# Edge counts of a four-layer graph network: windows of 64 destinations with source one-hots of 640 columns, interleaved with the first convolution's dense products

## The reference

```
h = max(layernorm(x), 0);  x = x + L0(h)     # one convolution: agg @ W_l.T + b_l + h @ W_r.T, relu
h = max(layernorm(x), 0);  x = x + L1(h)     # two convolutions of the same kind (mean over in-edges)
h = max(layernorm(x), 0);  x = x + L2(h)     # mean over out-edges, own layernorm inside
h = max(layernorm(x), 0);  x = x + L3(h)     # two GCN convolutions, self loops, 1/sqrt(degree)

agg = segment_sum(h[src], dst) / max(segment_sum(1, dst), 1)
```

## Time and profile before

| | |
|---|---|
| median of three executions | 733.56 us |
| span of the profiled execution | 731.7 us |
| TensorE busy | 706.2 us (97%) |
| VectorE busy | 433.6 us (59%) |
| ScalarE busy | 303.6 us (41%) |
| GpSimd busy | 31.0 us (4%) |
| counting and turning the counts | 13.9 to about 142 us |
| dense products of L0 | about 142 to 201 us |

### The profile page before, as it was taken

One profiled execution on the slowest core, in us unless ns is written; L12 is line 12 of the kernel. 1 busy time (PEld: TensorE's weight loads), 2 busy tenths in 40 slices (PEclk: granted clock), 3 DMA queues, 4 the chain that ended last, 5 costly groups with the idle time before them and its releaser, 6 DMA issues.

```text
span 731.7 us, 11918 instructions
## 1 busy us (share of the span) xinstructions
PE 706.2 (97%) x3435; PEld 551.0 (75%) x3436; DVE 433.6 (59%) x853; ACT 303.6 (41%) x613; POOL 31.0 (4%) x34
## 2 busy tenths in 40 slices
PE   3989999999999999999999999999999899999997
PEld 1545666688788888888888888888887678887786
DVE  5998999865456744422333466655699962247333
ACT  3887988522334222365311343222544352223321
POOL 1010111100000000000000000000222000000000
PEclk9999999999999999999999999999999999999999
DMA  7000000100012000011000201000200000000011
GB/s 245 5 1 15 20 24 30 57 0 0 2 59 73 0 0 1 6 69 58 0 0 1 74 4 54 1 0 0 74 0 0 2 2 0 1 0 0 32 57 54
DMA packets 12851, 18.68 MB, mean 26 GB/s; under 512 B 652, under 2 KB 5060, under 8 KB 12808
## 3 DMA queue, kind: packets, MB, share of 16 engines
q1 hardware_dynamic: 10472, 15.04, 6.3%
q10 hardware_dynamic: 2336, 3.08, 1.2%
HBM read 15.57 MB, written 2.56 MB: 25 GB/s over the span
## 4 chain that ended last, share of the span: by engine, by line
PE 78%; DVE 3%; issue 2%; ACT 1%; DVEq 0%; ACTq 0%
PE ps L1119 36%; PE ps L1161 36%; PE ps L1107 3%; PE ps L1063 2%; ACT cstage L485 1%; PE ps L1038 1%; PE ps L1022 0%; DVE own L890 0%; DVE countT L692 0%; DVE own L862 0%; DVE stats L658 0%; DVE own L795 0%; ACT apart L417 0%; DVE hT_lo L735 0%; DVE z L722 0%
## 5 line engine op out<-in xcount | busy, mean ns | idle before, releaser
L1161 PE MATMUL ps<-p_hi,cstage 128*128 128x512 f32 x600 | 234.5, 391 | 3.7 <-ACT cstage L485 2.0
L1161 PE MATMUL ps<-p_lo,cstage 128*128 128x512 f32 x600 | 233.6, 389 | 0.0
L1119 PE MATMUL ps<-w_hi,hT_hi 128*128 128x512 f32 x400 | 161.3, 403 | 2.1 <-DVE hT_lo L735 1.9
L1119 PE MATMUL ps<-w_hi,hT_lo 128*128 128x512 f32 x400 | 156.5, 391 | 0.0
L1119 PE MATMUL ps<-w_lo,hT_hi 128*128 128x512 f32 x400 | 156.0, 390 | 0.0
L1161 PEld LDWEIGHTS ps<-p_hi,cstage 128*128 128x128 f32 x600 | 112.6, 188 | 28.5 <-issue 5.3
L1161 PEld LDWEIGHTS ps<-p_lo,cstage 128*128 128x128 f32 x600 | 112.7, 188 | 23.1
L862 DVE SCALAR_TENSOR_TENSOR own<-ps,nodal,own 128x512 f32 (+1 forms) x60 | 44.9, 749 | 120.2 <-PE ps L1161 119.9
L1063 PE MATMUL ps<-src_hot,dst_hot 128*128 128x512 bf16 (+1 forms) x576 | 107.2, 345 | 6.3 <-DVE src_hot L675 5.4
L675 DVE TENSOR_SCALAR src_hot<-iota,nodeT 128x1250 bf16<-128x1250 f16 x192 | 94.2, 552 | 11.5 <-PE ps L1063 8.2
L485 ACT CAST cstage<-countT 128x1280 fp32r (+1 forms) x50 | 62.6, 1263 | 85.5 <-PE ps L1161 85.4
(11 more groups left out here) (124 smaller groups left out, 507.1 us busy)
## 6 DMA issues: line engine op xcount, KB each, us to landing
x<-in_x ACTq DMA_DIRECT2D x1, 2304.0 KB
out_x<-x SPq DMA_DIRECT2D x9, 256.0 KB
wstage<-in_L_gnn_W SPq DMA_DIRECT2D x2, 1024.0 KB, 5.2
vec<-in_L_gnn_b SPq DMA_DIRECT2D x4, 256.0 KB, 5.3
wstage<-in_L_gnn_W_r SPq DMA_DIRECT2D x4, 256.0 KB, 2.8
wstage<-in_L_gnn_W1l SPq DMA_DIRECT2D x1, 1024.0 KB, 5.1
wstage<-in_L_gnn_W1r SPq DMA_DIRECT2D x1, 1024.0 KB, 5.4
wstage<-in_L_gnn_W2l SPq DMA_DIRECT2D x1, 1024.0 KB, 5.3
```

Of the source, the lines that this page charges most:

```text
L1119: last = nc.tensor.matmul(ps[:, bank + r, :], a[:, r, k, :], w[:, slot, k, :], start=n == 0, stop=n == len(pairs) - 1)
L1161: last = nc.tensor.matmul(ps[:, AGG + r, :], cstage[:, part, k, :], p_[:, k, :], start=n == 1, stop=n == 2 * len(parts) * NT)
```

## The change

Six things change, all in the part up to the first aggregation.

1. Windows. Counting goes by 20 windows of 64 destinations (`WIN`, `NW`) instead of 10 blocks of 128. The sources are folded in two halves of 640: `src_hot` has 640 columns, and which half an edge belongs to goes into the sign of its destination, `(dst + 1) * (1 or -1)`. The 128 columns of `dst_hot` are then 64 destinations with the lower half of the sources and the same 64 with the upper half. TensorE multiplies two pieces of 320 columns. The minimum of two rounds to a block goes away; each window has at least one.
2. Who makes `dst_hot`. ScalarE makes the first three of a round (three `Abs`, one `Relu` over all three), GpSimd the last three with `is_equal` (`last_of_ring`).
3. Counts leave PSUM in four ScalarE activations of 64x640 to a block, straight into `count16`.
4. `countT16` is made by DMA: ten `dma_start_transpose` of 128x1280 on SyncE's queue, one when a block is complete. TensorE's and VectorE's share of the turning goes away. ScalarE and GpSimd wait for all ten before the first staging of an aggregation.
5. The two weights of L0 are loaded whole and transposed in two pieces of 16, before window 0 and between windows 0 and 1.
6. The products of L0 are interleaved: with block `b`, TensorE counts window 0, does the first product of tile `b-1`, counts window 1, transposes the features of tile `b` and does the second product of tile `b-1`.

```diff
-            def count(b, par, turned=None):
-                pe.wait_ge(counts_out, b + 1)
...
-                visits(n0, par)
-                if turned is not None:
-                    turn_counts(turned, par, GROUPS[2:])
-                    turn_first(turned, par)
...
+            def count(b, h, n1):
+
+                pe.wait_ge(counts_out, 2 * (2 * b + h) + 2)
...
+                with pe.Fori(n0, n1, RING) as n:
+                    for e in range(RING):
+                        if e == 0:
+                            pe.wait_ge(first_rows, n + 2 * RING)
+                        if e == HALF:
+                            pe.wait_ge(last_rows, n + 2 * RING)
+                        pe.wait_ge(givers_ready, n + e + 1)
+                        for k in range(2):
+                            last = nc.tensor.matmul(ps[:, COUNT + 2 * h + k, 0:NS // 2], dst_hot[:, e, :],
+                                                    src_hot[:, e, k * (NS // 2):(k + 1) * (NS // 2)], start=False,
+                                                    stop=False, skip_group_check=True)
+                        last.then_inc(hot_used, 1)
...
+            def merged(b, r):
+
+                n1 = visits_end(b)
+                count(b, 0, n1[0])
+                first_p(b - 1, 1 - r)
+                count(b, 1, n1[1])
+                turn(L0, b, r)
+                first_q(b - 1, 1 - r)
```

GpSimd's part, ScalarE's part and SyncE's transposes:

```diff
+            def last_of_ring(b, h, t0, t1, shift):
...
+                with pool.Fori(t0, t1, RING) as t:
+                    pool.wait_ge(last_rows, t + shift + RING)
...
+                    nc.gpsimd.tensor_copy(key_now[:, :], nodeT[:, 0, bass.ds(t + HALF, HALF)]).then_inc(key_set, RING)
+                    pool.wait_ge(key_set, t + shift + RING)
+                    pool.wait_ge(hot_used, t + shift + RING)
...
+                    for e in range(HALF):
+                        nc.gpsimd.tensor_scalar(dst_hot[:, HALF + e, :], tab_now[:, h, :], key_now[:, e:e + 1], None,
+                                                ALU.is_equal).then_inc(last_rows, 2)
...
+            def merged(b, r, first, second):
+
+                deviation(0, b)
+                receivers(b, 0, *first)
+                counts_of(b - 1, 1)
+                receivers(b, 1, *second)
+                phi(L0, b - 1, 1 - r)
+                counts_of(b, 0)
+                hi(L0, b, r)
...
+                if kind == "t":
+
+                    sp.wait_ge(counts_out, 4 * what + 8)
+                    sp.dma_start_transpose(countT16[:, :, what * P:(what + 1) * P], count16[:, what, :]
+                                           ).then_inc(cT_loaded, 16)
```

More of the change, by code:

```diff
@@ L219, in columns, with visits_of, window @@
         return (countT16 if CONVS[s]["by"] == "dst" else count16)[:, :, bass.ds(i * P, P)]
-    def visits_of(engine, b):
-        _, (t0, t1, shift) = nc.values_load_multi_w_load_instructions(
-            for_hots[0:1, bass.ds(b, 1), 0:3], engines=[engine.engine])
-        return nc.s_assert_within(t0, 0, ET - 1), nc.s_assert_within(t1, 2 * RING, ET + 2 * RING - 1), shift
-    assert 8 < NT <= 12
-    GROUPS = range(3)
+    IN_TABLE = "the table is clamped to the lists of edges, of ET tiles and of 3 * RING more that match no window"
+    def visits_of(engine, b, blocks):
+        _, found = nc.values_load_multi_w_load_instructions(
+            for_hots[0:1, bass.ds(2 * b, 2 * blocks), 0:3], engines=[engine.engine], bass_reorder=False)
+        return [(nc.s_assert_within(found[3 * w], 0, ET - 1, skip_runtime_bounds_check_because=IN_TABLE),
+                 nc.s_assert_within(found[3 * w + 1], RING, ET + 2 * RING - 1,
+                                    skip_runtime_bounds_check_because=IN_TABLE),
+                 found[3 * w + 2]) for w in range(2 * blocks)]
+    def window(b, h):
+        return bass.ds(2 * b + h, 1)
     def dma_rows(engine, dram, sbuf, sem_, store=False):
@@ L448, in _ @@
             act.wait_ge(table_step, steps_of_table)
[L449 to L465 removed]
+            act.wait_ge(pool_consts, 4)
             def hi(s, i, r):
@@ L796, in products, with merged @@
                                                    ALU.mult, ALU.add).then_inc(q_done, 1)
+            dve.wait_ge(nodes_placed, 1)
+            dve.wait_ge(pool_consts, 2)
+            found = visits_of(dve, 0, 2)
+            givers(*found[0])
+            split_first(0)
+            givers(*found[1])
+            split_first(1)
+            dve.wait_ge(x_loaded, 32)
+            statistics(0, 0)
+            features(L0, 0, 0)
+            statistics(0, 1)
+            lo(L0, 0, 0)
+            def merged(b, r, first, second, owned=True):
+                givers(*first)
+                if owned:
+                    first_own(b - 2)
+                features(L0, b, r)
+                givers(*second)
+                p_rest(L0, b - 1, 1 - r)
@@ new lines, in merged_end @@
+            def merged_end(b, r):
+                statistics(0, b + 1)
+                lo(L0, b, r)
+            merged(1, 1, *found[2:4], owned=False)
+            dve.wait_ge(vec_loaded[VSLOT[L0]], VCOUNT[L0])
+            merged_end(1, 1)
+            with dve.Fori(2, NT - 3, 2) as b0:
+                found = visits_of(dve, b0, 2)
+                for k in range(2):
+                    merged(b0 + k, k, *found[2 * k:2 * k + 2])
+                    merged_end(b0 + k, k)
+            found = visits_of(dve, NT - 2, 2)
@@ new lines, in _ @@
+            pe.wait_ge(dve_consts, 1)
+            pe.wait_ge(table_step, steps_of_table)
+            turn_first(0)
+            n1 = visits_end(0)
+            count(0, 0, n1[0])
+            turn_first(1)
+            count(0, 1, n1[1])
+            pe.wait_ge(wlo_done, 2 * KF)
+            turn(L0, 0, 0)
+            with pe.Fori(1, NT - 1, 2) as b0:
+                for k in range(2):
+                    merged(b0 + k, 1 - k)
+            merged(NT - 1, 1)
+            first_p(NT - 1, 1)
```

546 lines of the change are left out of this document (273 added, 273 removed).

## The result

The changed kernel took 741.17 us (median of four executions, 740.13 to 742.36) where the kernel before took 733.44 us on the same chip (four, 732.11 to 733.91): a ratio of 1.0116, interval 1.0098 to 1.0134. It is slower by about 1%. The forecast was 696 us, and its range did not hold the time.

What follows compares the result with a forecast made beforehand. TensorE was taken to bound the kernel, with GpSimd pacing multi-round windows; steps along TensorE's row put the aggregation at 163.5 instead of 201.1, span 694.1, plus 1.9: 696 us. Forecast range 688 to 704, over cases 682 to 722.

Steps and rivals of the forecast that it cites:

- until the first visit: Kernel start to first counting matmul: 14.2 us, with four new VectorE table steps and 16 weight transposes (1.8 us) ahead.
- into block 1: Gap after the first two windows, TensorE idle through splits, statistics, register reading and a first round: 9.8 us.
- blocks 2 to 4: Blocks of two-round windows: 13.3 us of TensorE work plus 1.0 and 0.4 of waits, 14.7 each.
- blocks 5 to 9: Five blocks of one-round windows between dense halves, 10.6 us each, including 1.4 of waits.
- tail: After the last counting: turn, second product of tile 8, both of tile 9, transposed maximum, hand-over to aggregation: 9.4 us.
- that is 3.2 us against TensorE's 3.1, plus 1.1 or more: Block starts: makers take 3.2 us against TensorE's 3.1, register reading adds 1.1 or more; 1.0 us of wait charged.
- registers 0.6: ScalarE's register reading in a block of one-round windows, 0.6 us of 8.5, covered by the two dense halves.
- so I take 0.36, near the select: GpSimd's 128x128 compare for `dst_hot`: 0.36 us each, 1.1 a round, setting multi-round windows' pace at 2.1 us.
- GpSimd is slower: Rival, chance 0.15: GpSimd compares at 0.6 us give 706 us in all, at 0.86 give 726.
- everything behind 201.10 keeps its instructions: From the first aggregation on, the program is unchanged; the only question is how much sooner it starts, 37.6 us.
- VectorE's one-hot at 0.30 us: In counting rounds, a source one-hot of 640 columns on VectorE takes 0.30 us, 1.8 us a round.
- the DMA transposes: Ten count transposes on SyncE's queue: 3.5 us each, hidden up to 6.4 us each, so nothing in the sum.

Runs made afterwards that it cites:

- experiment 11: Changed kernel with VectorE making the last three `dst_hot`, three vector loads moved later, registers read four values per block: 709.82 us, ratio 0.9688.
- Experiment 5: Changed kernel with each window's visits written in as constants and block loops unrolled, so no registers are read: 717.2 us, ratio 0.9788.
- Experiments 5 to 7: Changed kernel with constants for register reads, 717.2 us; that plus VectorE making the last three `dst_hot`, 694.57; constants plus slot-by-slot waits for GpSimd's buffers, 700.4.
- const: Changed kernel with visit lists as constants and block loops unrolled, reading no registers; the same run as Experiment 5: 717.2 us, ratio 0.9788.
- Experiments 9 and 10: Both const_dve3 kernels: with three vectors' loads moved behind the two next weights, 694.89 us; repeated without moving them, 694.55 us.
- const_dve3: const with VectorE instead of GpSimd making the last three `dst_hot` of a round: 694.57 us, ratio 0.9476.
- const_fill: const with eight matmuls of zeros in each round before TensorE's wait for GpSimd: 719.14 us, ratio 0.9808.
- best: The kernel of experiment 11, computing everything: VectorE's compares, vector loads moved, four register values read per block, against the changed kernel: 709.82 us.
- loads: ctl with registers read six values at a time instead of twelve, half of them later where engines wait anyway: 753.71 us, ratio 1.0283.
- ctl: Changed kernel with every register value that is read tested against bounds: 777.89 us, ratio 1.0619.

## Why the forecast was wrong

Each step of the sum, against the changed kernel:

| step | forecast us | measured us |
|---|---|---|
| until the first visit | 14.2 | 16.5 |
| window 0 | 13.8 | 20.2 |
| between the windows | 2.9 | 1.9 |
| window 1 | 6.0 | 8.5 |
| into block 1 | 9.8 | 8.8 |
| block 1 | 10.3 | 14.8 |
| blocks 2 to 4 | 44.1 | 61.7 |
| blocks 5 to 9 | 53.0 | 61.0 |
| tail | 9.4 | 12.3 |
| start of the aggregation | 163.5 | 205.7 |

Two terms carry nearly all of it.

*The registers.* The step that failed is "that is 3.2 us against TensorE's 3.1, plus 1.1 or more on the engine that reads registers [...] I put 1.0 for that". I took the price from the old kernel's "issue", where an engine reads three values; the changed one reads twelve in one go. Both kernels' own rows, before and then after (duration ns min/median/max):

```profile
L223 ACTq TENSOR_LOAD <-for_hots x10: 694/703/912, 10.5 to 126.4; - x10
```

```profile
L243 ACTq TENSOR_LOAD <-for_hots x6: 961/2644/2674, 11.9 to 182.6; - x6
L243 DVEq TENSOR_LOAD <-for_hots x5: 873/2785/2825, 11.8 to 173.4; - x5
L243 POOLq TENSOR_LOAD <-for_hots x5: 2760/2784/3602, 12.0 to 168.3; - x5
```

Three values take 0.70 us (ScalarE; VectorE 0.76), twelve 2.64 to 2.79 in the median: 0.22 to 0.25 us a value, so the price could have been read off the old trace once the values of an instruction were counted. One thing does not fit a price per value. VectorE's readings at 11.8 and 173.4 fetch twelve values too and took 1.12 and 0.87 us (the smallest figure of its row). They stand outside the loop over blocks, at a place in the table that is fixed in the program; in experiment 11 four values took 0.31 to 0.60 us outside the loop and 0.93 to 1.02 inside. But ScalarE's last six, also outside, took 1.33. What makes a reading cheap is open; a kernel that unrolls the loops and still reads would tell, and was not tried. And I expected cover: "registers 0.6" in blocks 5 to 9, within two dense halves. But the chain of waits through each boundary is one dependency, from the engine that reads, over a first one-hot, to TensorE's next visit; what stands beside it covers nothing. Experiment 5 prices the whole of it at 28.6 us, lower clock and the loops' own control included. The slow matmuls in it (12.2 us of 26 in the long stretch) I had allowed for only at the kernel's start.

*GpSimd's compare.* "so I take 0.36, near the select" failed. It takes:

```profile
L361 POOL TENSOR_SCALAR dst_hot<-tab_now,key_now x105: 597/605/1541, 16.4 to 189.6; 128x128 bf16<-128x128 f16 x105
```

The structure of the round was right: compares, two hand-overs and three visits. With the measured terms it is 2.20 + 0.13 + 0.26 + 0.92 = 3.51 where I had 1.1 + 0.2 + 0.82 = 2.1. Nor is it mostly contention, for which I had left room by the cast of the earlier trace rows. With VectorE idle for nearly all of it three of them still take 1.76:

```profile
72.43 1.76 POOL L361 TENSOR_SCALAR dst_hot<-tab_now,key_now 128x128 bf16<-128x128 f16 x3 [0.23 <-POOL key_now L356]
...
75.38 3.64 DVE L742 TENSOR_SCALAR src_hot<-iota,nodeT 128x640 bf16<-128x640 f16 x12 [2.69 <-issue]
```

So 0.59 alone, 0.73 beside VectorE. A select of the same size at 0.29 was the wrong neighbour. The rival "GpSimd is slower" was the right one of the four; it gave 706 for 0.6 and 726 for 0.86, with the pace of 0.86 (3.6 a round) being nearly the one that came (3.51), though a compare takes 0.73; the kernel's 741 is above both, since the rival left the registers as they were. Experiments 5 to 7 price it at 18.2 us, of which 12.3 come from its wait for the whole round. Without both causes the aggregation starts at 158.8, 4.7 us ahead of the 163.5 of the forecast.

The smaller steps. The first visit came late since the 16 transposes waited for the weight and then took 3.65 us and not 1.8, half the rate of the old chunks of the earlier trace rows, though the granted clock of 12 to 20 us reads 1.00 (the same riddle as the earlier trace rows):

```profile
12.94 3.65 PE L1117 MATMUL ps<-ident,wstage 128*128 128x128 f32 x16 [1.90 <-DMA wstage<-in_L_gnn_W_l]
```

Part of the tail's 2.9 us and the 2.9 us that the rest of the program grew by lie around the aggregation's start. There the chain reads, and behind it stand the changed kernel's and const's waits for "issue" at the start of an aggregation:

```profile
202.27 1.26 ACT cstage L509
203.53 2.12 issue
205.65 9.47 PE ps L1243 x28
...
PE ps L1243 <- issue: 3.1, 1, 3.1
...
PE ps L1236 <- issue: 7.8, 3, 2.9
```

The staged counts are there at 203.53, and TensorE begins at 205.65, after 3.06 us of standing idle. Experiments 9 and 10 have this gap too, at 2.65 and 3.29 us, where before it was 0.47; what fills it was not found. Nor was the rest of the program as free of the change as "everything behind 201.10 keeps its instructions" suggests: it takes 530.6 us before, 533.5 in the changed kernel (granted clock 0.78 from 205 to 220), 693.3 - 158.8 = 534.5 in const_dve3 and 715.3 - 177.04 = 538.3 in const, whose clock reads 1.00 from 177 to 192. Most of const's excess has a place: the same kind of wait comes back at the start of two later aggregations, 2.92 us at 284.82 and 1.99 at 585.48, and the 50 us around each have a granted clock of 0.97; the changed kernel and const_fill (717.6 - 184.83 = 532.8) have neither. Why a kernel has these waits or not stays open. They are why starts were compared above and not only times.

Right were: VectorE's one-hot at 0.30 us (six in 1.86 to 1.92 us where nothing held them up); ScalarE's share, never the last in a round that follows another; and the DMA transposes. The 9.8 us into block 1 (8.8) were right by luck: the reading in them took 2.67 for 1.1, and the other terms together 2.6 less than forecast. For the transposes I took 3.5 us by size and got 3.4. The Trainium skill was divided on them: of its two statements, "VectorE: DVE Perf Modes", the three transpose paths, gives a figure for one 128x128 from which I had estimated 13 us for these ten times larger ones, and the trace contradicts that estimate (no single 128x128 was run); "Advanced Engine Details and Errata", X-Bar Transpose, has them as fast as plain transfers, and the trace agrees, as far as 3.4 us against 3.5 scaled from a plain load can show it.

## What to carry to other kernels

Count the values that a register read fetches and price each from a trace (here 0.23 us inside the loops); reading belongs behind an engine's own slack, and slack must be looked for again after every move of work onto that engine. When TensorE's share shrinks, look first at which order of waits closes the loop between consumer and makers: waiting slot by slot gave 12 of the 18 us that a slow maker cost, without making it faster. Idle time on TensorE can be paid more than once, since matmuls behind it may run at the lower clock (12.2 us beside 13.8 of idle time in experiment 5); look at the granted clock of the stretch before counting on it.

## What the runs showed of the hardware

- Reading values into registers inside a loop, medians: three 0.70 to 0.76 us, four 0.93 to 0.99 (in best), six 1.35 to 1.44 (in loads), twelve 2.64 to 2.79. VectorE's two readings of twelve outside the loop took 1.12 and 0.87. Bounds tests follow one another every 0.27 us on VectorE's sequencer and twelve take 2.7 us on ScalarE's (in ctl).
- GpSimd compares 128x128 of 16 bits with a scalar in 0.60 us (0.73 beside VectorE's one-hots in window 0), VectorE in 0.24, at a pace of 0.17.
- A DMA transpose of 128x1280 two-byte values within SBUF landed 3.4 us after its issue, and issuing took 1.34 us of the queue.
- Waits of TensorE of 1.7 us in rounds of 3.5 left the granted clock at 1.00 (16.5 to 36.75 us); behind boundaries with gaps of over 2 us it fell to 0.50 for 100 to 105 us, and twelve dense matmuls took 3.61 to 4.28 us in place of 2.81. Not every such gap did it: behind 2.89 us before 177.04 in const the clock read 1.00 (177 to 192 us).
